# Router logits of a two-layer router: weights held in the array by column quarters, activations streamed

## What is computed

```python
logits = jax.nn.silu(jnp.einsum('bsd,dh->bsh', x, rw1) + rb1)
logits = jnp.einsum('bsh,he->bse', logits, rw2) + rb2
k_logits, k_index = jax.lax.top_k(logits, TOPK)
k_prob = jax.nn.softmax(k_logits, axis=-1)
...
for e in range(E):
    we = jnp.sum(jnp.where(k_index_f == e, k_prob_f, 0.0), axis=-1)
    h = jax.nn.silu(xf @ w1[e] + b1[e]) @ w2[e] + b2[e]
    out = out + we[:, None] * h
```

## Time and profile before

| | us |
|---|---|
| median of 3 runs | 386.02 (385.85 to 386.42) |
| the profiled execution, first to last instruction | 388.5 |
| PE busy in it | 309.1 (80%) |
| POOL, DVE, ACT busy in it | 174.2, 194.7, 133.3 |

### The profile page before, as it was taken

How to read it: one execution, slowest core, us unless ns; L and a number is a source line. 1 busy time by engine, 2 the same in 40 slices (tenths; PEclk the granted TensorE clock), 3 DMA queues, 4 the chain that set the end, 5 groups by cost and what they waited for, 6 DMA issues and landing times.

```text
span 388.5 us, 6416 instructions
## 1 busy us (share of the span) xinstructions
PE 309.1 (80%) x1736; PEld 242.7 (62%) x1737; DVE 194.7 (50%) x791; ACT 133.3 (34%) x267; POOL 174.2 (45%) x188
## 2 busy tenths in 40 slices
PE   0295839999999999710799999999999999999200
PEld 0252415669667865710588888888888888888200
DVE  3879899773677722240243333333343333432187
ACT  1049989322322242000243333433344333443000
POOL 1806282087576855762044444444444444444300
PEclk9999877866868786555599999999999999999755
DMA  7950000011010111114322212222211212200398
GB/s 227 324 172 14 0 2 2 0 37 49 29 54 29 50 41 50 41 62 117 83 54 59 58 54 61 61 67 56 56 47 45 69 41 61 60 29 13 86 321 241
DMA packets 41635, 28.39 MB, mean 73 GB/s; under 512 B 5463, under 2 KB 38273, under 8 KB 41616
## 3 DMA queue, kind: packets, MB, share of 16 engines
q1 hardware_dynamic: 32498, 17.56, 16.4%
q0 software_dynamic: 4544, 8.47, 6.7%
q10 hardware_dynamic: 4574, 2.13, 1.9%
HBM read 16.39 MB, written 12.67 MB: 75 GB/s over the span
## 4 chain that ended last, share of the span: by engine, by line
PE 73%; DVE 11%; ACT 5%; DMA 4%; SPq 3%; issue 3%; POOL 1%; POOLq 0%; DVEq 0%
PE bank L897 19%; PE bank L885 18%; PE bank L833 11%; PE bank L845 10%; PE bank L877 4%; PE bank L899 3%; PE bank L856 3%; PE bank L771 2%; DMA xs<-in_L_attn_x_dram 1%; DMA av<-expert_out 1%; DVE st L521 1%; PE bank L858 1%; SPq L315 1%; ACT hT L436 1%; SPq L307 1%
## 5 line engine op out<-in xcount | busy, mean ns | idle before, releaser
L412 POOL DMA_INDIRECT expert_out<-tx,dest_t x78 | 76.8, 985 | 109.3 <-DVE tx L738 102.8
L494 ACT ACTIVATE tx<-bank,w_t 128x256 f32<-128x256 f32 x156 | 65.0, 471 | 129.9 <-PE bank L885 129.2
L897 PE MATMUL bank<-w_s,tx 128*128 x624 | 86.4, 281 | 0.0
L401 POOL DMA_INDIRECT sorted_rows<-rows,sloti x64 | 64.1, 1002 | 39.5 <-DVE sloti L647 22.4
L897 PEld LDWEIGHTS bank<-w_s,tx 128*128 128x128 f32 x624 | 78.6, 191 | 4.6
L885 PE MATMUL bank<-h2T,w_t 128*128 128x256 f32 x312 | 75.9, 387 | 0.0
L738 DVE TENSOR_SCALAR tx<-bank,prob_t 128x128 f32<-128x128 f32 x78 | 27.3, 350 | 80.5 <-PE bank L899 80.5
L885 PEld LDWEIGHTS bank<-h2T,w_t 128*128 128x128 f32 x312 | 57.6, 195 | 6.8 <-DVE w_t L730 0.3
L833 PE MATMUL bank<-h2T,rw_s 128*128 128x512 f32 x64 | 45.7, 881 | 0.8 <-ACT h2T L467 0.8
L724 DVE COPY h2T<-bank 128x256 f32<-128x256 f32 x39 | 16.6, 424 | 44.2 <-PE bank L877 34.0
L877 PE MATMUL bank<-ident,tx 128*128 128x128 f32 x78 | 17.7, 310 | 19.9 <-DMA tx<-sorted_rows 19.9
(11 more groups left out here) (158 smaller groups left out, 343.6 us busy)
## 6 DMA issues: line engine op xcount, KB each, us to landing
tx<-sorted_rows SPq DMA_DIRECT2D x39, 130.0 KB, 2.2
w_s<-in_L_ffn_w_dram SPq DMA_DIRECT2D x16, 256.0 KB, 5.9
xs<-in_L_attn_x_dram SPq DMA_DIRECT2D x8, 256.0 KB, 4.6
av<-expert_out SPq DMA_DIRECT2D x8, 256.0 KB, 4.9
qv<-expert_out SPq DMA_DIRECT2D x8, 256.0 KB, 5.7
expert_out<-tx,dest_t POOLq DMA_INDIRECT x78, 2.3
sorted_rows<-padr SPq DMA_DIRECT2D x9, 130.0 KB, 2.6
sorted_rows<-rows,sloti POOLq DMA_INDIRECT x64, 2.3
```

Source lines behind the costliest of these rows:

```text
L401: p.indirect_dma_start(sorted_rows[:, :], bass.IndirectOffsetOnAxis(ap=sloti[:, k, t:t + 1], axis=0), rows[:, t, k, :], None).then_inc(s_d ...
L412: p.indirect_dma_start(expert_out[:, :], bass.IndirectOffsetOnAxis(ap=dest_t[:, s % U, n, :], axis=0), yo[:, s % 2, n, :], None, bounds_ch ...
L494: ins = nc.scalar.activation(hsT[:, u % 2, h, :], bank[2 + 2 * (u % 2) + q][:, (h % 2) * SL:(h % 2 + 1) * SL], ACT.Silu, bias=w1_t[:, u % ...
L897: t.matmul(o, hsT[:, u % 2, h, n * P:(n + 1) * P], w2_s[:, bass.ds(e * (HC * D) + h * D, D)], start=(h == 0), stop=False)
```

## The change

The logits are computed with the roles of the operands exchanged, and in two steps. In `logits` each quarter of rw2 (128 hidden units x 8 experts, widened to 32 columns with zeros, `QP = 32`) is the weights and the quarter of `hr` is streamed whole, 512 columns. The four quarters write four different groups of 32 partitions of bank 5. A new part `lgc` on ACT copies bank 5 to `lgT`. A new part `sum` on PE then uses each 128 x 128 piece of `lgT` as weights and streams `sum4`, a 128 x 8 matrix of ones and zeros that adds the four partials and puts tokens on the partitions again, as the result in bank 6 was before.

```diff
@@ logits on PE @@
             def logits(g):
+
                 pe.wait_ge(s_hr, HC * (g + 1))
+                for h in range(HC):
+                    ins = t.matmul(bank[5][h * QP:(h + 1) * QP, :], rw2_s[:, h, :], hr[g % 2][:, h, :],
+                                   start=True, stop=True)
+                ins.then_inc(s_lgT, 1)
+
+            def logit_sums(g):
+
+                pe.wait_ge(s_lgTc, g + 1)
                 if g == 0:
 
                     pe.wait_ge(s_modrow, 1)
+                    pe.wait_ge(s_sum4, 1)
                 else:
                     pe.wait_ge(s_lgc, g)
                 for j in range(GT):
-                    for h in range(HC):
-                        ins = t.matmul(bank[6][:, j * NE:(j + 1) * NE], hr[g % 2][:, h, j * P:(j + 1) * P],
-                                       rw2_s[:, h, :], start=(h == 0), stop=(h == HC - 1))
+                    ins = t.matmul(bank[6][:, j * NE:(j + 1) * NE], lgT[:, g % 2, j * P:(j + 1) * P],
+                                   sum4[:, :], start=True, stop=True)
                 ins.then_inc(s_lg, 1)
@@ router on PE @@
+                    if g and h == HC - 1:
+
+                        pe.wait_ge(s_lgTc, g)
@@ ACT @@
+            def logit_copy(g):
+                act.wait_ge(s_lgT, g + 1)
+                if g >= 2:
+                    act.wait_ge(s_lg, g - 1)
+                nc.scalar.copy(lgT[:, g % 2, :], bank[5][:, :]).then_inc(s_lgTc, 1)
+
             def router_silu(g):
                 if g >= 2:
-                    act.wait_ge(s_lg, g - 1)
+                    act.wait_ge(s_lgT, g - 1)
@@ POOL, SP and DVE, at the start @@
+            p.memset(rw2_s[:, :, :], 0.0).then_inc(s_zero, 1)
...
+            sp.wait_ge(s_zero, 2)
+            sp.dma_start(rw2_s[:, :, 0:NE], rw2.rearrange("(c p) e -> p c e", p=P)).then_inc(s_rw, 16)
...
+                dve.wait_ge(s_ident, 1)
+                v.tensor_reduce(sum4[:, :], ident[:, :].rearrange("p (q e) -> p e q", e=QP)[:, 0:NE, :],
+                                AX.X, ALU.add).then_inc(s_sum4, 1)
@@ ACT's order: one line of several @@
-                decay:7 dup:0 copy:0 mult:1 silu:0 copy:1 copy:2 dup:1 dup:2 silu:1 share:0 dup:3 silu:2 share:1 copy:3
+                decay:7 dup:0 copy:0 mult:1 silu:0 copy:1 copy:2 lgc:0 dup:1 dup:2 silu:1 share:0 dup:3 lgc:1 silu:2
```

More of the change, by code:

```diff
@@ L43, in adaln_block @@
     U = 4
+    QP = 32
     TILES = (TOPK * TOK + NE * (SL - 1)) // SL
@@ L68, in adaln_block @@
         rw1_s = sb("rw1_s", [P, HID])
-        rw2_s = sb("rw2_s", [P, HC, NE])
+        rw2_s = sb("rw2_s", [P, HC, QP])
+        sum4 = sb("sum4", [P, NE])
+        lgT = sb("lgT", [P, 2, G])
         w1_s = sb("w1_s", [P, NE * WE])
@@ L202, in adaln_block @@
         s_y01 = sems(*(f"s_y01_{g}" for g in range(NG)))
+        s_sum4, s_lgT, s_lgTc = sems("s_sum4", "s_lgT", "s_lgTc")
         rows_i = rows[:, :, :, :].bitcast(I32)
@@ L220, in adaln_block @@
                 gates:4 gates:5 turn_x:6 turn_x:7 turn_y:0 gates:6 turn_y:1 gates:7 turn_y:2 turn_h:0 router:0 turn_y:3
-                turn_h:1 turn_h:2 logits:0 router:1 rank:0 turn_y:4 logits:1 router:2 rank:1 turn_h:3 logits:2 turn_y:5
-                router:3 rank:2 turn_h:4 logits:3 turn_y:6 router:4 rank:3 turn_h:5 logits:4 turn_y:7 router:5 rank:4
-                turn_h:6 logits:5 router:6 rank:5 turn_h:7 logits:6 router:7 rank:6 logits:7 rank:7""",
+                turn_h:1 turn_h:2 logits:0 router:1 sum:0 rank:0 turn_y:4 logits:1 router:2 sum:1 rank:1 turn_h:3 turn_y:5
+                logits:2 router:3 sum:2 rank:2 turn_h:4 turn_y:6 logits:3 router:4 sum:3 rank:3 turn_h:5 turn_y:7
+                logits:4 router:5 sum:4 rank:4 turn_h:6 logits:5 router:6 sum:5 rank:5 turn_h:7 logits:6 router:7
+                sum:6 rank:6 logits:7 sum:7 rank:7""",
             "vector": """
@@ L233, in adaln_block @@
                 modulate:4 modulate:5 mult:0 tanh:4 modulate:6 tanh:5 modulate:7 decay:4 tanh:6 decay:5 tanh:7 decay:6
-                decay:7 dup:0 copy:0 mult:1 silu:0 copy:1 copy:2 dup:1 dup:2 silu:1 share:0 dup:3 silu:2 share:1 copy:3
-                dup:4 silu:3 share:2 copy:4 silu:4 share:3 copy:5 dup:5 silu:5 share:4 dup:6 copy:6 silu:6 share:5
-                copy:7 dup:7 silu:7 share:6 share:7""",
+                decay:7 dup:0 copy:0 mult:1 silu:0 copy:1 copy:2 lgc:0 dup:1 dup:2 silu:1 share:0 dup:3 lgc:1 silu:2
+                share:1 copy:3 lgc:2 dup:4 silu:3 share:2 copy:4 lgc:3 silu:4 share:3 copy:5 lgc:4 dup:5 silu:5
+                share:4 copy:6 lgc:5 dup:6 silu:6 share:5 copy:7 lgc:6 dup:7 silu:7 share:6 lgc:7 share:7""",
             "gpsimd": """
@@ L291, in _ @@
             sp.dma_start(rw1_s[:, :], rw1).then_inc(s_rw, 16)
-            sp.dma_start(rw2_s[:, :, :], rw2.rearrange("(c p) e -> p c e", p=P)).then_inc(s_rw, 16)
+            sp.wait_ge(s_zero, 2)
+            sp.dma_start(rw2_s[:, :, 0:NE], rw2.rearrange("(c p) e -> p c e", p=P)).then_inc(s_rw, 16)
             sp.dma_start(rb2_row[:, :], rb2.rearrange("(a e) -> a e", a=1)).then_inc(s_rw, 16)
@@ L343, in _ @@
             p.memset(half_neg[:, :], -0.5).then_inc(s_const, 1)
-            pool.wait_ge(s_zero, 1)
+            p.memset(rw2_s[:, :, :], 0.0).then_inc(s_zero, 1)
+            pool.wait_ge(s_zero, 2)
             p.affine_select(out=ident[:, :], in_=ident[:, :], compare_op=ALU.not_equal, fill=1.0,
@@ L372, in constants @@
                 p.memset(before[:, :], 1.0).then_inc(s_zero, 1)
-                pool.wait_ge(s_zero, 2)
+                pool.wait_ge(s_zero, 3)
                 p.affine_select(out=before[:, :], in_=before[:, :], compare_op=ALU.is_gt, fill=0.0,
@@ L385, in constants @@
                 p.memset(padr[:, :, :], 0.0).then_inc(s_zero, 1)
-                pool.wait_ge(s_zero, 3)
+                pool.wait_ge(s_zero, 4)
                 p.iota(padr_i[:, :, D + 1], pattern=[[P, HALVES]], base=TOPK * TOK,
@@ L485, in _ @@
             run("scalar", {"modulate": modulate, "tanh": gates, "decay": decay, "mult": multiplier,
-                           "copy": router_copy, "dup": duplicate, "silu": router_silu, "share": second_share})
+                           "copy": router_copy, "dup": duplicate, "silu": router_silu, "lgc": logit_copy,
+                           "share": second_share})
             def hidden(s, u):
@@ L863, in _ @@
                            "gates": gate_products, "turn_y": y_transpose, "turn_h": h2_transpose,
-                           "router": router, "logits": logits, "rank": ranks})
+                           "router": router, "logits": logits, "sum": logit_sums, "rank": ranks})
             pe.wait_ge(s_slot, NG)
```

## The result

The changed kernel takes 398.1 us (median of 4 runs, 394.58 to 400.56) against 386.2 us of before (4 runs, 385.85 to 389.74). The ratio is 1.024 (95% interval 1.017 to 1.032): slower, by 11.9 us between the medians, as forecast. Two later pairs of runs on other occasions gave 1.016 (1.011 to 1.021) and 1.019 (1.014 to 1.025), so the size is better told as 6 to 12 us. The two profiled spans, 388.5 and 396.8 us, differ by 8.3 us, and it is this difference that the traces can account for. Executions of one kernel fall into faster and slower ones, and each ratio is taken over the faster ones alone, so it can differ by some tenths of a per cent from the quotient of two medians.

The account below looks back on a forecast made before the run. PE's work was taken to bound the middle stage; -38.4 + 17.2 + 9.6 + 16.7 + 7.9 + 0.8 - 1.9 = +11.9 us on 386.0 gave 397.9 us, range 385 to 410.

Parts of the forecast that it names:

- The wait for the masks: Middle stage, sum right ahead of rank: PE idles 2.39 us for top2's masks in seven more groups, +16.7 us.
- The wait for the scan: Turns now ahead of the logits: turn_y:6 and 7 wait 3.6 us each for DVE's scan; with small waits +7.9 us.
- the two small waits: Middle stage: turn_y:5 waits 0.3 us for inputs and scan, turn_h:6 waits 0.4 us for norm2:6.
- The logits: Middle stage: old logits go, -38.4 us; new quarters take five records, 2.15 us a group, +17.2 us; chance 0.45.
- all at once: Rival on the new logits: all four quarters overlap, 0.86 us a group, 6.9 us for eight, 387.6 us; chance 0.13.
- The routers: Middle stage: no clock fall in group 1's router, -1.9 us; the other routers stay at their 5.7 us mean.
- Ranks and turns: Middle stage: the work of ranks 0 to 6 and of the turns was forecast to change by 0.
- the clock stays up: Rival on the stage's clock: it no longer falls, routers shrink to 3.44 us each, 16.3 us off, 381.6 us; chance 0.11.
- Sums, copy and the way to the experts: Sums +9.6 us, group 7's wait for the bank 5 copy +0.8 us, last rank to experts' first load unchanged.

Follow-up runs that it names:

- sum_ahead_again: Second run of the changed kernel with the sum ahead of the router and the turns back behind the logits: 371.9 us, 0.958 of the kernel before.
- turn_back_again: Second run of the changed kernel with only turn_y:5 to 7 put back behind the logits: 1.007 of the kernel before.
- turn_back: First run of the changed kernel with only turn_y:5 to 7 put back behind the logits: 1.008 of the kernel before.
- one_group: The changed kernel with all four logits quarters in one column group, adding into the same 32 partitions: 417.2 us, 1.071 of the kernel before.
- fill_wait: The changed kernel with two added 512-column matmuls between sum and rank in each group: 1.004 of the kernel before.
- sum_ahead: First run of the changed kernel with the sum ahead of the router and the turns back behind the logits: 0.990 of the kernel before.
- split_router: First run of the changed kernel with the sum after the router's first quarter and the other three behind it: 0.980 of the kernel before.
- the first set: The changed kernel again (1.016), sum_ahead, turn_back and split_router, run together with the kernel before, which took 397.0 us there.

## Why the prediction was right, point by point

The sign, the reason and the predicted time held (397.9 against 398.1 us). But the traces account for only 8.3 us, and the repeated pairs for 6 to 8 us, so the closeness of the median is in part luck: terms were mis-sized in both directions.

**The wait for the masks** (+16.7 us): measured +16.8, eight waits of 2.4 us. The one row of before with that neighbourhood gave the size exactly. That the sum's place is the cause is shown by sum_ahead_again, which leaves two of the eight waits, is 20.0 us faster than turn_back_again with nothing else changed, and comes out 4% under the kernel before. More than the wait itself goes with it, since the clock rises too.

**The wait for the scan** (+7.9 us): the place was right, the size not; measured 1.99 + 2.58 = 4.6 us for turn_y:6 and 7, and next to nothing for the two small waits (0.3 and 0.4 us) beside them. DVE's chain from the masks to the scan's end came as worked out (117.42 to about 123.3, 5.9 us; forecast 6.0). What was off is what PE does meanwhile: rank and turn take 3.3 us after and not 2.4, because of the clock (117.42 to 119.66, and 1.09 for the turn). Most of the time did not vanish; it stands in the table as the work of ranks and turns. turn_back and turn_back_again gave back 4.8 us.

**The logits**: the forecast put five records into a group, 2.15 us at full clock; it is two and a little, 1.00 us. The step that failed was the argument that the second record of a quarter holds back the next quarter: it does not. The rival "all at once" (0.86 us a group) had the mechanism right, and it had a chance of only 0.13. The total still came near (14.1 against 17.2 us), because the forecast charged full clock, and seven of the eight groups ran at 1.2 GHz and took 1.9 us each. Two errors of opposite sign, and no virtue of the estimate. By the span model of the Trainium skill (TensorE: Matmul & The Clock Gate, Part 3, Measured speedup vs the span model), the time of one tile and about 4 ns for each further one, a group would take 0.87 us, an estimate from that page with the 0.86 us of two records; the trace has 1.00 us, near it. The speedup of 2.38 that the same table lists is for three column tiles, 0.79 a tile; one_group's 3.55 us against 1.00 us is a factor of 3.5 for four, 0.89 a tile. The drain that the Trainium skill warns of (TensorEngine Tiling (Array Packing), Key Properties) can be at most what is left over two records, 1.00 - 0.86 = 0.14 us, and what the turn ahead of the logits takes longer, 0.10 to 0.16 us: some 0.3 us a group, and no run tells it from other costs of the same size.

**The routers** (-1.9 us): measured -8.1. The forecast left them their mean of 5.7 us and with it their cold head. But that head moved: the stretch at 1.2 GHz, which before began during the logits or just behind them and ended in the router (in group 1 from 70 to 73 us), now begins at the rank and ends in the router, and the new logits lie inside it. The routers after take 3.53 us in group 1, as forecast, and 4.0 to 5.1 in the others. What they gained, logits, ranks and turns lost. The forecast left the clock in one part's mean instead of writing it as an account of its own, and so had both entries wrong.

**Ranks and turns** (0): measured +3.4 and +3.7 us. This is the term that the forecast did not have. Before, a rank ran straight behind a router at full clock, 1.88 us; after, it stands behind 2.4 us of idle PE, the clock falls at its head or in its course, and it takes 2.1 to 2.75 us. fill_wait shows the cause: with the idle time filled, the rank at 114.33 takes 1.88 us and the turn behind it 0.64 us again. A small part of the turns' growth is not the clock but the place ahead of the new logits, as said under the table.

**The rival "the clock stays up"** did not come true in the changed kernel (0.75 in the stage, 0.74 before). fill_wait comes nearest to it: with the clock at 0.89, and the time of the waits now spent on the filler, the ratio is 1.004, still not faster than before.

**Sums, copy and the way to the experts** came as worked out: 8.6 us for 9.6, 0.7 for 0.8, and 23.4 us in both.

**What stays open.** The standstill of about 8 us in sum_ahead and split_router, and the longer way from the last rank to the experts in all four traces of the first set (27.3 to 31.5 us in place of 23.4), in which several of SP's instructions took 0.70 us each. Neither came back in the later sets, and no experiment aimed at the cause. The 1.6 us that the experts take more after, the 3.5 us between the two traces of the kernel before, and the spread of the ratio between the three pairs (1.016 to 1.024), are not explained either.

## What to carry to other kernels

Cheaper products do not help if the new order puts a product, the vector step on it and the product that needs this step right behind each other: count the distance between them on the engine, and put other work there, which here turned a loss of 2% into a gain of 4%. Charge a wait on PE twice, once for itself and once for a slower clock of what stands behind it, which here made up about half of the 25 us, and keep the clock in an account of its own and not in the mean of one part. When such a stage gets faster, look for the engine that is next: here it is POOL, whose row of sends holds up the small normalisation step that other engines wait for.

## What the runs showed that was not expected

- Four float32 matmuls of 512 columns in four column groups of 32 take 1.00 us at full clock and 1.87 at half; in one column group 3.55 us at full clock. In four groups both records of every quarter overlap with the others.
- Added work can make the kernel faster: two matmuls a group in the place of a 2.4 us wait, clock 0.75 to 0.89, 4.5 to 8 us gained.
- A stage's pace passed to POOL at 1.26 us a send (0.96 us busy, 0.30 us of issue), 86 us for 64 sends with the steps between them, and it reached PE through one 1.0 us step queued behind the sends.
- In some executions three engines stood still for 8 us while POOL's sends went on, with PE's semaphore updates 9 us late.
